# Feed-forward halves and the out bias moved to GpSimd, one branch on VectorE, and a new order of all five engines

## The reference

```python
x = layernorm(x + attention(x))        # 16 heads of 16, 4 key heads, causal
x = layernorm(x + wkv(k=x, v=ctx))     # recurrence over 128 steps, per channel
x = layernorm(x + ffn(x))              # 256 -> 1024 -> 256, sign weights
```

## Time and profile before

| | |
|---|---|
| runs, median | 178.46 us (177.83 to 178.72) |
| span of the profiled execution | 178.1 us, 3837 instructions |
| TensorE busy (modelled) | 157.8 us, 1388 matmuls |
| VectorE busy | 156.5 us, 289 instructions |
| ScalarE busy | 138.9 us, 280 instructions |
| GpSimd busy | 83.4 us, 109 instructions |
| granted TensorE clock, mean | 0.979 |

### The profile page before, as it was taken

How to read it: one execution, slowest core, us unless ns; L and a number is a source line. 1 busy time by engine, 2 the same in 40 slices (tenths; PEclk the granted TensorE clock), 3 DMA queues, 4 the chain that set the end, 5 groups by cost and what they waited for, 6 DMA issues and landing times.

```text
span 178.1 us, 3837 instructions
## 1 busy us (share of the span) xinstructions
PE 157.8 (89%) x1388; PEld 107.8 (61%) x1388; DVE 156.5 (88%) x289; ACT 138.9 (78%) x280; POOL 83.4 (47%) x109
## 2 busy tenths in 40 slices
PE   7978769989999999999999999999969798999920
PEld 2445424545645645566886668769758687898810
DVE  1489679798789999999899999999999999999981
ACT  3745488988998889999899989696687897898700
POOL 8282601017404695020873623699679457270121
PEclk9999969999999999999999999999999999999995
DMA  5899039044709107941070310000300010001122
GB/s 175 244 320 392 5 62 209 2 92 75 249 0 95 56 2 94 212 127 48 0 151 0 75 48 2 0 4 0 118 0 4 0 59 0 36 27 61 63 79 107
DMA packets 17989, 14.65 MB, mean 82 GB/s; under 512 B 12656, under 2 KB 13616, under 8 KB 17712
## 3 DMA queue, kind: packets, MB, share of 16 engines
q1 hardware_dynamic: 17424, 13.87, 29.8%
q10 hardware_dynamic: 544, 0.50, 0.9%
HBM read 9.52 MB, written 2.10 MB: 65 GB/s over the span
## 4 chain that ended last, share of the span: by engine, by line
PE 48%; DVE 27%; ACT 10%; issue 8%; DMA 3%; POOL 2%; SPq 0%; POOLq 0%; DVEq 0%; ACTq 0%
PE banks L417 9%; PE banks L576 8%; PE banks L500 7%; PE banks L597 6%; PE banks L533 5%; DVE hid_lo L1760 5%; DVE state L1702 4%; PE banks L472 4%; ACT probs L971 3%; DMA probs<-biases_dram 3%; DVE ratio L1712 2%; DVE stats L1676 2%; PE banks L510 2%; ACT dn_sb L918 2%; PE banks L479 2%
## 5 line engine op out<-in xcount | busy, mean ns | idle before, releaser
L971 ACT ACTIVATE probs<-banks 128x1024 f32<-128x1024 f32 x32 | 31.8, 1022 | 4.8 <-PE banks L479 4.8
L597 PE MATMUL banks<-dn_sb,hid_hi 128*128 128x256 bf16 x128 | 29.1, 272 | 1.1 <-DVE hid_lo L1760 1.1
L576 PE MATMUL banks<-x2hi,up_sb 128*128 128x256 f16 x128 | 29.1, 273 | 0.8 <-DVE x2lo L1753 0.5
L597 PE MATMUL banks<-dn_sb,hid_lo 128*128 128x256 bf16 x128 | 29.1, 273 | 0.0
L576 PE MATMUL banks<-x2lo,up_sb 128*128 128x256 f16 x128 | 29.0, 272 | 0.0
L417 PE MATMUL banks<-wqkv_sb,xT_sb 128*128 128x384 f32 x64 | 23.5, 512 | 2.0 <-issue 1.6
L1355 POOL TENSOR_SCALAR veps<-stats 128x2 f32<-128x2 f32 x24 | 9.4, 394 | 27.8 <-DVE stats L1676 26.8
L1361 POOL TENSOR_TENSOR rstd<-veps,half_neg 128x2 f32<-128x2 f32 x24 | 20.4, 853 | 1.3
L1019 ACT ACTIVATE banks<-banks,ups_man 128x256 f32<-128x256 f32 x48 | 19.6, 470 | 1.8 <-PE banks L576 1.6
L417 PEld LDWEIGHTS banks<-wqkv_sb,xT_sb 128*128 128x128 f32 x64 | 12.4, 201 | 11.9 <-issue 3.4
L1702 DVE TENSOR_TENSOR_SCAN state<-dec_sb,ke 128x1032 f32<-128x1032 f32 x8 | 18.4, 2301 | 0.0
(11 more groups left out here) (129 smaller groups left out, 355.8 us busy)
## 6 DMA issues: line engine op xcount, KB each, us to landing
ctxT_sb<-ctxT_dram SPq DMA_DIRECT2D x8, 256.0 KB, 3.1
x_sb<-x_dram SPq DMA_DIRECT2D x8, 256.0 KB, 3.8
out_dram<-outb SPq DMA_DIRECT2D x8, 256.0 KB, 2.2
xT_sb<-xT_dram SPq DMA_DIRECT2D x7, 256.0 KB, 4.4
up_f<-up_dram SPq DMA_DIRECT2D x1, 1024.0 KB, 6.4
dn_f<-down_dram SPq DMA_DIRECT2D x1, 1024.0 KB, 8.4
wqkv_sb<-wqkv_dram ACTq DMA_DIRECT2D x2, 192.0 KB, 3.1
xT_sb<-xT_dram SPq DMA_DIRECT2D x2, 128.0 KB, 2.9
```

The source lines that it names most:

```text
L576: mm = nc.tensor.matmul(banks[:, UP[p][n], s * T * S:(s + 1) * T * S], up_sb[:, c, j * 128:(j + 1) * 128], part[:, c, :, :].rearrange("p t ...
L597: mm = nc.tensor.matmul(banks[:, DN[p], t * D:(t + 1) * D], part[:, t * S:(t + 1) * S], down_of(j), start=(j == 0 and t == 0 and m == 0), ...
L971: nc.scalar.activation(probs[:, (T * p + t) % PROBS_N, 2 * h:2 * h + 2].rearrange("p n j s -> p n (j s)"), banks[:, b:b + 2], ACT.Exp).the ...
```

## The change

The out bias is no longer three bfloat16 rows in a product: `bo_b` holds it in all partitions, and GpSimd's `add_bias(p)` adds it to `x_sb` ahead of `residual(p)`. VectorE has one branch, with the whole order in two copies. GpSimd gets `high_bits` (13 of 32 calls) and has 23 of 32 `low_bits` (before 5); table HID says which groups lie in SBUF. The two float16 parts of x2 are one tensor `x2T`, double-buffered, with the sequence outside the channel half. The last pair's down product goes to two banks, its last group is done in two halves, and scaling, adding and storing follow by halves. The q, k, v bias is loaded as three rows into a cleared buffer, and the gains are loaded by SP. The order of calls and the tables of banks are new on all engines; of the orders only the first part of ScalarE's, GpSimd's middle and the ends are shown.

```diff
+        bo_b = sb("bo_b", [128, D])
-        x2hi = sb("x2hi", [128, NC, T, S], F16)
-        x2lo = sb("x2lo", [128, NC, T, S], F16)
+        x2T = sb("x2T", [128, X2T_N, 2, T, NC, S], F16)
...
-            hi_done="AGGGGAGA",
-            lo_done="VGVVGGGG",
-            stack_done="AVAAAAAA",
-            kv_done="VGVVGVGG",
-            lo2_done="GGGVGGVV",
+            hi0_done="AAGGAGAG",
+            hi1_done="GAGGAAAA",
+            hi2_done="GGGAAGAA",
+            hi3_done="AAAGAGAA",
+            hi_done="GGGGGAGA",
+            lo0_done="GVGGGGGV",
+            lo1_done="GGGGGGVV",
+            lo2_done="VVGGGVGG",
+            lo3_done="GGGGGGVV",
+            lo_done="VVGGGGGG",
+            stack_done="VAVVVAVV",
...
+        HID = ((1, 0, 0, 1), (1, 0, 1, 0), (1, 0, 1, 0), (0, 0, 1, 0), (0, 1, 0, 1), (0, 1, 0, 1), (0, -1, 0, -1), (0, -1, 1, -1))
...
-        params = [(tdec[:], decay_in), (tfirst[:], first_in), (ups_sb[:], up_s),
+        params = [(bo_b[:], bias_out.partition_broadcast(128)), (tdec[:], decay_in), (tfirst[:], first_in), (ups_sb[:], up_s),
...
@@ sync
-            sp.dma_start(bias_in[:, 0:E], biases[0:E].partition_broadcast(BR)).then_inc(bias_in_done, 16)
+            sp.wait_ge(bias_clear, 1)
+            for r in (0, 32, 64):
+                sp.dma_start(bias_in[r:r + 1], biases.partition_broadcast(1)).then_inc(bias_in_done, 16)
+            for dst, src in gain_loads:
+                sp.dma_start(dst, src).then_inc(gains_in, 16)
...
+            store_half(7, 0)
+            store_half(7, 1)
@@ tensor
-                nc.tensor.matmul(banks[:, WO[p]], ones_b[:], bias_rows[:, E:E + D].unsqueeze(1).to_broadcast([BR, T, D]),
-                                 start=True, stop=False)
...
+            def ffn_down_half(p, t):
+
+                n = NJ // 2 - 1
+                hidden_there(p, n)
+                for s in range(2):
+                    j = 2 * n + s
+                    for m, part in enumerate((hid_hi, hid_lo)):
+                        mm = nc.tensor.matmul(down_tile(p, t), part[:, j, t * S:(t + 1) * S], dn_sb[:, j],
+                                              start=False, stop=(s == 1 and m == 1))
+                mm.then_inc(sems["dn_mm"], 1)
...
             project(1)
-            pe.wait_ge(masks_ready, MASKS)
-            pe.wait_ge(guard_ready, GUARDS)
+            project(2)
+            done(pe, "rot_done", 0)
+            project(3)
+            first_rows()
             pe.wait_ge(gain_ready, GAINS)
             plain = pe.value_load(flags[0:1, 0:1], min_val=0, max_val=1)
@@ scalar, the first part of the order
             masks()
+            decay_rates()
             squares(0)
             take_values(0)
+            down_signs()
+            mean_log(0)
+            squares(1)
+            first_root(0)
+            now_gains()
+            up_signs()
             take_values(1)
-            mean_log(0)
-            first_root(0)
-            squares(1)
-            high_heads(0)
+            down_weights(0)
+            take_values(2)
+            down_weights(1)
+            take_values(3)
+            first_rows_out()
             mean_log(1)
             first_root(1)
             squares(2)
...
@@ gpsimd
+            def add_bias(p):
+
+                landed(pool, "x_in", p)
+                if p == 0:
+                    pool.wait_ge(params_in, PARAMS)
+                rows_of = x_sb[:, p % X_N]
+                nc.gpsimd.tensor_tensor(rows_of, rows_of, bo_b[:].unsqueeze(1).to_broadcast([128, T, D]), ALU.add)\
+                    .then_inc(sems["xb_done"], 1)
+            def high_bits(p, n):
+
+                done(pool, "hid_done", p, 2 * n + 2)
+                nc.gpsimd.tensor_copy(hid_hi[:, 2 * n:2 * n + 2], hidden(p, n)).then_inc(signal(f"hi{n}_done", p), 1)
...
+            high_bits(2, 0)
+            low_bits(1, 3)
+            low_bits(2, 0)
+            high_bits(2, 1)
+            den_by_rec(4)
+            low_bits(2, 1)
+            high_bits(2, 2)
+            inverse_root(0, 6)
+            low_bits(2, 2)
+            add_out(1)
...
@@ vector
+            plain = dve.value_load(flags[0:1, 0:1], min_val=0, max_val=1)
+
+            def from_heads(guarded):
+
+                small_constants()
+                head_sums(0)
+                rope_sines(0)
...
+                scale_half(7, 0)
+                add_half(7, 0)
+                scale_half(7, 1)
+                add_half(7, 1)
+                moments(2, 7)
+                landed(dve, "stored", 4)
+                normed(2, 6)
+                landed(dve, "stored", 5)
+                normed(2, 7)
```

More of the change, by code:

```diff
@@ L400, in _ @@
             store(6)
[L401 to L403 removed]
+            store_half(7, 0)
+            store_half(7, 1)
+            landed(sp, "stored", PAIRS - 3)
+            landed(sp, "stored", PAIRS - 2)
+            sp.wait_ge(last_stored, 16 * T)
         @block.tensor
@@ L1074, in _ @@
-            up_signs()
-            swap_keys(2)
+            first_root(4)
+            squares(5)
             exps(1, 1, 0)
-            now_gains()
+            exps(1, 1, 1)
             take_channels(0)
-            mean_log(4)
-            squares(5)
-            first_root(4)
-            exps(1, 1, 1)
+            mean_log(5)
+            first_root(5)
             take_products(1, 0)
-            swap_keys(3)
+            done(act, "pv_mm", 1)
+            take_values(5)
             take_products(1, 1)
-            take_values(5)
@@ L1809, in _ @@
-            head_sums(3)
-            with dve.If(guarded):
-                row_maxima(1)
-            low_heads(2)
-            small_constants()
-            rope_sines(4)
-            rope_cosines(4)
-            rope_sum(4)
-            newton_rms(3)
-            attend_norm(0)
-            scale_heads(3)
-            head_sums(4)
-            low_heads(3)
-            newton_rms(4)
-            residual(0)
-            moments(0, 0)
-            with dve.If(guarded):
-                row_maxima(2)
@@ L1827, in _ @@
-            done(dve, "rscale_done", 4)
-            head_sums(5)
-            rope_sines(5)
-            attend_norm(1)
-            rope_cosines(5)
-            normed(0, 0)
-            rope_sum(5)
-            newton_rms(5)
-            keys_by_context(0)
-            scan(0)
-            residual(1)
-            mix(0)
-            with dve.If(guarded):
-                row_maxima(3)
-            moments(0, 1)
-            rope_sines(6)
-            rope_cosines(6)
-            attend_norm(2)
@@ L1863, in _ @@
-            offsets(1, 0)
-            rope_cosines(7)
-            rope_sum(7)
-            scan(1)
-            with dve.If(guarded):
-                row_maxima(5)
-            residual(3)
-            mix(1)
-            low_x2(0)
-            newton_rms(7)
-            keys_by_context(2)
-            attend_norm(4)
-            moments(0, 3)
-            num_by_rec(1)
-            scale_heads(7)
-            scan(2)
-            refine(1)
-            low_bits(0, 0)
-            done(dve, "ny_done", 1)
```

1308 lines of the change are left out of this document (667 added, 641 removed).

## The result

The changed kernel takes **211.4 us** (median of 4 runs, 210.7 to 212.2) against 178.3 for the kernel before beside it (177.8 to 178.7): a ratio of 1.184, 95% interval 1.179 to 1.189. It is 33 us slower where 3 us of gain were forecast, and outside the range. The profiled execution has a span of 209.5 us.

A forecast was written before the change was run, and what follows sets the result against it. VectorE was taken as the bound from 130 to 140 us, TensorE waiting; +6.0 start, -2.7 bias products and rounding, -0.7 and -4.4 stalls, -1.3 tail = -3.1, giving 175.4 us, range 171.0 to 181.5.

The forecast's parts named there:

- GpSimd against VectorE: VectorE instructions with two SBUF inputs and GpSimd ones exclude each other; more GpSimd work costs +3 us, between 0 and +8.
- rival A: Behind attend_norm(3), the SBUF port shared by VectorE and GpSimd decides: slower, run 180.6 us; chance 0.18.
- Start: Later parameters and dn_f delay ScalarE's mean_log(0); scores(0,0) starts at 27.8, not 21.8: +6.0 us, bounds +3.5 and +7.5.
- Stalls before scores(4,0): TensorE's stalls from scores(0,0) to scores(4,0): 4.5 us where 5.2 were, -0.7.
- my walk: New order walked from scores(0,0) on: TensorE reaches scores(4,0) at about 65.9 us, with 4.5 of stalls.
- Stalls behind it: TensorE's stalls behind scores(4,0), set by VectorE: 4.4 us where 8.8 were, -4.4.
- Tail: From the last matmul to the end, last group in two halves: 6.3 us instead of 7.6, -1.3.
- Out bias: Eight bias products of 0.33 leave TensorE, -2.6 us; eight additions, 9.4 us, come to GpSimd.
- VectorE's work: VectorE's whole order falls from 152.8 to 141.2 us, from scan(0) on from 116.0 to 104.0; busy 144 to 149.
- Median and span: The runs' median stands 0.4 us above the profile's span, so a span of 175.0 becomes 175.4.
- sign of rival A: GpSimd instructions of 1.2 us stretched to 2 and more throughout, with VectorE's two-input ones at over 1.2.

## Why the prediction was wrong

**The step that failed** is the one on GpSimd against VectorE: "In proportion that is 5.1, so +2.5; I take +3, between 0 (an order without collisions) and +8 (rival A)". All of GpSimd's reads measured 27.3; less the 2.6 that the forecast counted for the kernel before, some 25 stand against its +3. The mechanism was named, with the rows that show it, and rival A was this one; its size was off, eight times. Three things were wrong in it.

- *The rate.* 2.6 us of blocks over the 36 large GpSimd instructions of before, 44 us, is 0.07 each, and I took it for the rate of those to come. It was the rate of instructions in chosen places. Added reads cost 0.36 us (18 reads) and 0.35 (13.6 over 39) of time in the same order, over memsets of the same length, and more in VectorE's excess. The bias alone cost 0.39 (3.1 over 8), queue included and TensorE's relief taken off.
- *The kind of work.* The step weighed how much GpSimd reads, not what VectorE was rid of: 18 subtractions with an input in PSUM, which do not collide.
- *The reads that were there already.* They keep their places only while the order stands. By the GpSimd instruction that lies beside each stretched one, 19.6 of the 36.3 us fall to low_bits (12.7, five of its 23 there before), add_bias (4.8) and high_bits (2.1), and the other 16.7 to work that had made 3.0 before, and to six other reads that moved with it.

Rival A's 180.6 assumed that VectorE and GpSimd would fill each other's gaps and lose only what doesn't fit. Both take their orders in sequence: a 0.07 us offset waits 1.2 us, and what stands behind it waits too. Its sum was also off by its own terms: 93.1 - 39.6 leaves VectorE 53.5 us of other work, not 46.5, so by its rule the surplus would have been 1.1 us, not 8. Its direction was right and its time far short.

The other steps, against the profile (209.5 = 29.1 + 132.0 + 10.2 + 30.9 + 7.3, by the forecast's terms: start, work, stalls up to scores(4,0), stalls behind, tail; without GpSimd's reads 28.3 + 132.0 + 8.4 + 6.5 + 7.2 = 182.4):

- *Start:* +7.3 for +6.0, inside its bounds and by the chain named: ScalarE waits for dn_f until 18.34 (17.7 forecast), mean_log(0) at 20.16 (19.6). It matters little, as the run with the start back showed (1.6 us).
- *Stalls before scores(4,0):* 10.2 for 4.5. 1.8 of it goes with the reads. The other 3.9 are off in my walk, which took everything at full clock: up to 3.4 us of the 10.2 are the granted clock of 0.50 from 29.1 to 35.8 (before, from 24.0 to 27.5, 1.7 at the most). The forecast had at most 1 us for that, and only in its range.
- *Stalls behind it:* 30.9 for 4.4; 6.5 without reads. VectorE is late and TensorE stands or, for up to 5 us of it, runs at half speed behind such stands.
- *Tail:* 7.3 for 6.3. I counted 0.8 us of half-size scale and add behind the last matmul; it is 1.4 (202.2 to 203.57), since the second half's scale queues behind the first half's add. By itself the edit gains nothing.
- *Out bias:* "-2.6" on TensorE was real and worth nothing; it cost 3.1.
- *VectorE's work:* right to a few us. 149.5 us busy without GpSimd's reads, with about 8 of excess beside memsets in it.
- *Median and span:* I added 0.4, what the median of before stands above its profile's span. In every run whose time and span are both on record the time is 1.8 to 2.5 us above the span (211.4 to 209.5). So the profile of before was probably of an execution some 1.5 us slower than the median, and the account in spans above falls 1.5 us short of the miss in time.

So 27.3 of the 36.0 us missed (211.4 - 175.4) go with the reads; without any, the kernel would still have missed by 8.7.

The sign of rival A that the forecast gave came in part: single GpSimd instructions at 2 us and more and two-input ones of VectorE at over 1.2, but not throughout; the means are 1.48 for GpSimd's low halves and 1.14 for the mix.

## What to carry to other kernels

Before moving work from VectorE to GpSimd, sort VectorE's instructions by operands. Those with two SBUF inputs, or scaling from SBUF to SBUF, take turns with GpSimd's reads nearly as on one engine. An instruction with an input in PSUM collides with nothing as long as it stays on VectorE; moved to GpSimd it becomes a read that does. Few collisions in a profile tell of the order, not of the price: price an added read by what it displaces where it lands (here 0.36 us of time each, 0.58 with the longer queue), and expect a new order to lose the places of the old reads too. To test it, turn the suspected reads into memsets of the same length.

## What was not expected of the hardware

- An idle gap of GpSimd is no free place: additions put into gaps of 1.3 us and more cost VectorE 1.06 us of excess each, 0.6 of it beside the additions.
- Copies from SBUF to float16 at 0.33 us never gave way: a GpSimd addition took 3.05 us in place of 1.27, held up by all six.
- GpSimd's memsets stretch VectorE's scaling from SBUF (0.46 to 0.72) and nothing else of the table, so a memset is not a wholly neutral stand-in.
- A GpSimd power of 128x2 (0.69) blocks next to nothing (0.60 to 0.64 beside it), so the roots themselves are harmless; what follows them is not.
